# A recurrent layer with an FFN gate on one core: the gate computed in the preparation, and each super-tile finished inside the next one

## The chip, the cores and the metric

The kernel runs on one core of one Trainium2 chip. A core has four compute engines that run side by side and meet at semaphores: TensorE (PE; its weight loads are listed as PEld), VectorE (DVE), ScalarE (ACT) and GpSimd (POOL); SyncE (SP) issues the DMA transfers here. SBUF and PSUM are its memories. The metric is the time of the whole program on the device in microseconds (us); the median of three runs is given.

## The reference

The input x is (4, 1024, 128), 4096 tokens of 128 features. All is float32.

```python
xn = layernorm(x)
s  = attn(xn)                       # H=32 heads, P=64, N=64, DI=2048
x  = x + s * silu(ffn(xn))

# attn
proj = u @ in_proj_w.T              # z, xin, B, C, dt, theta, lambda
Bm = rms(Braw) * w + B_bias         # per head; Cm likewise
tc = cumsum(theta, axis=1)          # over the tokens
Bm, Cm = rope(Bm, tc), rope(Cm, tc) # v1*cos - v2*sin, v1*sin + v2*cos
h  = a_t * h + g_t * (x_t B_t) + b_t * (x_{t-1} B_{t-1})   # per head, a scan
y  = h C_t + xh * D
y  = rms(y * silu(z)) * norm_w
return y @ out_proj_w.T

# ffn: both operands through fp8 with one scale for each tensor
fake_quant(t) = fp8(t * 448 / max|t|) * max|t| / 448
ffn = fake_quant(xn) @ fake_quant(weight).T + bias
```

The gate needs the largest magnitude of the whole of xn. The RMS norm of y runs over all 32 heads of a token, and it is a factor per token behind the output projection.

## The kernel before, in words

The 4096 tokens are cut into 8 super-tiles (t) of 512 tokens, a super-tile into 4 chunks of 128. The 32 heads go in 8 groups (q) of 4 heads; each group is two pairs (p). Three functions run one after the other, each a block with a barrier at its end; inside a block each engine has its own list of instructions, in the order in which they are written.

`prepare` (stage 1) normalises x, transposes it (`xnT`) and the weights, takes the running sum of xn over the tokens (`tcT`, since the angle is linear in it), and computes B and C, the decays and the per-token factors (`kk`, `cc`, `dec`, `cum`). `xnT`, `tcT`, B/C and the decays are stored to DRAM (`xn_t`, `tc_t`, `bc_t`, `cum_parts`, `cum_rows`). VectorE works through chains of whole-width operations (L484 to L543); ScalarE makes the transposed B/C (L604), the logarithms and exponentials (L615 to L628) and the casts (L635 to L643).

`units` (stage 2) is the recurrence, 64 rounds (t, q). For each:
- angle: TensorE `angles` (L825), ScalarE `rounding` (L1122), VectorE `angles` (L1000) to a fraction of a turn; ScalarE `sines` (L1126 to L1133) fill `tri`, and SP's `spread` (L774), eight DMAs, lays them out over the partitions of `trig`. This is done for round q + 2 during q, and a spread of pair p waits until VectorE has read the old `trig`.
- rotation (L1026): eight VectorE operations, each (B or C + bias) x (cos or sin); GpSimd's `sums` (L1189) add them in pairs to `rot`. This is done one round ahead.
- TensorE transposes the rotated B (L836), makes exponents (L846, L853), scores (L864), states (L916), x (L830), z (L944), y (L950 to L966) and the output projection (L878), which adds up over q in one PSUM bank, `Op`. ScalarE exponentiates (L1138, L1160), applies Silu to z (L1164) and squares (L1143); VectorE scales x (L1010), masks scores (L1044), updates the state (L1075), multiplies y by silu(z) (L1103) and decays B (L1036); GpSimd makes `ce` (L1198) and adds the squares over the heads in `sqa` (L1220).
- At the end of a super-tile TensorE sums `sqa` over the features (L987) into the bank `Dp`; ScalarE copies `Op` to `s_acc` (L1175) and the sums to `ssq` (L1177). At q = 2 VectorE takes the largest and the smallest of this super-tile's xn (`mags`, L1109).
- Before the first round, angles, sines and spreads for q = 0 and 1 are made with nothing beside them.

`finish` (stage 3) turns `mags` into the fp8 scales, `ssq` into 1/rms, and passes over the 8 super-tiles again: xn and x are loaded, ScalarE scales xn twice (L1309, L1310), VectorE rounds it to fp8 in five steps (`quantise`, L1363 to L1369), TensorE multiplies with the weight, VectorE adds the bias (L1389), ScalarE takes tanh (L1315), VectorE completes Silu and multiplies (L1395, L1398), GpSimd scales `s_acc` (L1407) and adds x (L1415), and SP stores the result.

## Time and profile before

| | us |
|---|---|
| median of 3 runs | 1339.04 (1335.22 to 1344.77) |
| the profiled execution | 1338.07 |
| its span, first to last instruction | 1336.3 |

| engine | busy us | share of the span |
|---|---|---|
| VectorE | 1224.1 | 92% |
| TensorE, matmuls | 1133.7 | 85% |
| TensorE, weight loads | 832.9 | 62% |
| ScalarE | 797.7 | 60% |
| GpSimd | 728.3 | 55% |

Each engine's busy time is its instructions' time added up; an average over the three stages hides that they have different limits. The last stage runs from 1271.7 on, the first up to 98.0.

### The profile page before, as it was taken

How to read it: one execution, taken by the hardware profiler on the slowest of the kernel's cores; microseconds unless marked ns; L12 is line 12 of the kernel's file. 1: busy time of each engine (PE TensorE's matmuls, PEld its weight loads, DVE VectorE, ACT ScalarE, POOL GpSimd, SP SyncE). 2: the span in 40 equal slices, each digit the busy share in tenths (PEclk: the TensorE clock that was granted, in tenths of full speed). 3: DMA queues.
4: the chain of work that ended last, by engine and by line, in shares of the span. 5: the costliest groups of instructions: out<-in, count | busy, mean ns of one | idle time of the engine just before them, and what ended most of it. 6: DMA issues, size and time to landing. Idle time of an engine off the chain costs nothing. (4 is left out here: it accounts for less than half of the span.)

```text
span 1336.3 us, 30910 instructions
## 1 busy us (share of the span) xinstructions
PE 1133.7 (85%) x11514; PEld 832.9 (62%) x11514; DVE 1224.1 (92%) x1945; ACT 797.7 (60%) x1226; POOL 728.3 (55%) x562
## 2 busy tenths in 40 slices
PE   4873999989999999999999999899999999999810
PEld 3742666666666666666676666666766666667600
DVE  7774999989998999999998999899989999999688
ACT  5732666656666666666666666666666666666432
POOL 4001566656665566556664666566655665666523
PEclk9865999999999999999999999999999999999955
DMA  7535332343221422342223323342224323222033
GB/s 185 176 98 127 73 73 65 69 93 85 65 65 44 106 66 66 68 112 66 63 63 74 81 66 68 66 113 57 60 51 112 66 65 69 61 57 60 19 100 89
DMA packets 68513, 105.66 MB, mean 79 GB/s; under 512 B 14051, under 2 KB 32716, under 8 KB 68044
## 3 DMA queue, kind: packets, MB, share of 16 engines
q1 hardware_dynamic: 68364, 103.68, 33.2%
q8 instruction: 93, 1.52, 0.5%
q14 instruction: 56, 0.46, 0.1%
HBM read 24.73 MB, written 9.96 MB: 26 GB/s over the span
## 5 line engine op out<-in xcount | busy, mean ns | idle before, releaser
L1189 POOL TENSOR_TENSOR rot<-part 128x512 f32<-128x512 f32 x256 | 382.5, 1494 | 531.9 <-DVE part L1026 480.4
L1026 DVE SCALAR_TENSOR_TENSOR part<-bcs,k_prmT,trig 128x512 f32<-128x512 f32 x512 | 500.5, 1028 | 1.4 <-DMA trig<-tri 1.3
L1138 ACT ACTIVATE E<-d 128x512 f32<-128x512 f32 x256 | 151.7, 592 | 184.1 <-PE d L846 181.5
L864 PE MATMUL s<-rot 64*128 64x128 f32 x2048 | 149.7, 285 | 23.6 <-POOL rot L1189 19.1
L1044 DVE TENSOR_TENSOR M<-s,E 128x512 f32<-128x512 f32 x256 | 163.5, 678 | 2.4 <-PE s L864 1.8
L864 PEld LDWEIGHTS s<-rot 64*128 64x128 f32 x2048 | 126.9, 188 | 62.0 <-issue 54.6
L1198 POOL TENSOR_TENSOR ce<-rot,eb 128x512 f32<-128x512 f32 x128 | 160.1, 1272 | 3.0 <-ACT eb L1160 3.0
L1220 POOL TENSOR_TENSOR sqa<-sqa,sq 128x512 f32<-128x512 f32 x112 | 142.5, 1272 | 14.2 <-ACT sq L1143 6.2
L956 PE MATMUL y<-M,xk 128*64 128x128 f32 x2048 | 140.1, 279 | 0.0
L878 PEld LDWEIGHTS o<-k_w_o,yT 128*128 128x128 f32 x1024 | 132.5, 191 | 10.4 <-DVE yT L1103 5.0
L878 PE MATMUL o<-k_w_o,yT 128*128 128x128 f32 x1024 | 134.5, 275 | 2.6 <-DVE yT L1103 2.6
L830 PE MATMUL r<-k_w_zx,xns 128*128 128x256 f32 x512 | 133.2, 382 | 3.3 <-DVE ang L1000 3.3
L944 PE MATMUL r<-xns,k_w_zx 128*128 128x512 f32 x256 | 122.6, 596 | 4.2 <-DVE xc L1010 4.2
L956 PEld LDWEIGHTS y<-M,xk 128*64 128x64 f32 x2048 | 109.2, 136 | 21.5 <-issue 21.5
L825 PE MATMUL r<-tcs,k_w_th 128*128 128x512 f32 x128 | 73.9, 660 | 56.6 <-DVE bw L1036 42.3
L1160 ACT ACTIVATE eb<-d 128x512 f32<-128x512 f32 x128 | 76.5, 597 | 68.4 <-PE d L853 68.4
L1164 ACT ACTIVATE sz<-r 128x512 f32<-128x512 f32 x128 | 76.4, 597 | 61.1 <-PE r L944 60.9
L1143 ACT ACTIVATE sq<-yT 128x512 f32<-128x512 f32 x128 | 80.0, 625 | 48.9 <-DVE yT L1103 48.9
L1010 DVE TENSOR_TENSOR xk<-r,k_kk 128x512 f32<-128x512 f32 x128 | 88.0, 688 | 22.6 <-PE r L830 22.0
L830 PEld LDWEIGHTS r<-k_w_zx,xns 128*128 128x128 f32 x512 | 96.9, 192 | 15.8 <-issue 4.8
L846 PE MATMUL d<-k_cum,k_pick 111*128 111x512 bf16 x256 | 99.6, 389 | 0.0
L916 PEld LDWEIGHTS r<-xk,bw 128*64 128x64 f32 x1792 | 57.5, 137 | 50.7 <-DVE bw L1036 44.4
(234 smaller groups left out, 1792.8 us busy)
## 6 DMA issues: line engine op xcount, KB each, us to landing
trig<-tri SPq DMA_DIRECT2D x512, 128.0 KB, 2.4
bcs<-bc_t SPq DMA_DIRECT2D x16, 256.0 KB, 4.0
bcs<-bc_t SPq DMA_DIRECT2D x32, 128.0 KB, 3.9
a_big<-in_L_attn_u SPq DMA_DIRECT2D x4, 512.0 KB, 6.0
xn_t<-a_xnT SPq DMA_DIRECT2D x1, 2048.0 KB, 16.4
tc_t<-a_tcT SPq DMA_DIRECT2D x1, 2048.0 KB, 15.9
bc_t<-a_tmp SPq DMA_DIRECT2D x1, 2048.0 KB, 7.5
tcs<-tc_t SPq DMA_DIRECT2D x8, 256.0 KB, 3.0
```

What stands on the lines that cost most here:

```text
L830: last = nc.tensor.matmul(R[i][:, 256 * c:256 * c + 256], xns[:, (t + q // NQ) % 2, (2 * i + c) * P:(2 * i + c + 1) * P], K["w_zx"][:, DI ...
L846: nc.tensor.matmul(Dp[:], K["pick"][:, head * P:head * P + P], K["cum"][0:D_ROWS, q % 2, h, :], start=True, stop=True).then_inc(d_ready, 1)
L864: last = nc.tensor.matmul(Sp[j][:, k], rot[rows, q % 2, p, 0, k], rot[rows, q % 2, p, 1, k], start=True, stop=True)
L878: last = nc.tensor.matmul(Op[:, k], yT[:, p, k], K["w_o"][:, (2 * q + p) * P:(2 * q + p + 1) * P], start=False, stop=q == NQ - 1 and c == ...
L944: nc.tensor.matmul(R[p][:], w, xns[:, t % 2, :], start=True, stop=True).then_inc(z_ready, 1)
L956: nc.tensor.matmul(Yp[p][m:m + 64, k], xk[:, par, c, 128 * p + m:128 * p + m + 64], M[:, 2 * p + j, k], start=False, stop=c == 0 and begin ...
L1026: nc.vector.scalar_tensor_tensor(out=part[:, 2 * p + f, :], in0=bcs[:, (t + q // NQ) % 2, 2 * w + f, :], scalar=col, in1=trig[:, p, 1 - f, ...
L1044: nc.vector.tensor_tensor(M[:, h, :], Sp[h % 2][:], E[:, h % 2, :], ALU.mult).then_inc(m_ready, 1)
L1138: nc.scalar.activation(E[:, h % 2, :], Dp[:], ACT.Exp).then_inc(e_ready, 1)
L1189: nc.gpsimd.tensor_tensor(rot[:, q % 2, p, w, :], part[:, 2 * p, :], part[:, 2 * p + 1, :], ALU.add).then_inc(rot_ready, 1)
L1198: nc.gpsimd.tensor_tensor(ce[:, p, :], rot[:, q % 2, p, 1, :], eb[:, p, :], ALU.mult).then_inc(ce_ready, 1)
L1220: nc.gpsimd.tensor_tensor(sqa[:], sqa[:], sq[:, p, :], ALU.add).then_inc(sqa_ready, 1)
```

## The change

- **Gate in `prepare`.** VectorE takes the largest and the smallest of `xnT` (`extreme`, eight reductions over 1024 columns) and of the FFN weight, and makes the scales (`sc`). ScalarE scales xn (`gate_input`), VectorE quantises (`quantise`, the same five steps), TensorE multiplies, with the bias put in as a first matmul, and ScalarE applies Silu directly. The eight gates are stored to DRAM (`gate_rows`) at the end of the stage.
- **Angles of q = 0 and 1 in `prepare`.** Two matmuls on `tcT`, rounding, fraction and sines; group 0 is also spread. `rnd` shares memory with `tcT`, so the first rounding waits until `tcT` has been stored (`stored[1]`).
- **`units` starts with the loads of B/C**; the first rotations come ahead of the scaling of x.
- **`units` finishes super-tile t - 1 during t.** At q = 0: VectorE reads the sums of squares (`norm_start`), ScalarE takes the root (`root`), VectorE the reciprocal (`norm_seeded`), GpSimd refines it (`norm_refined`), ScalarE copies `Op` with the factor for each token (`normalised`). At the end of q = 1 GpSimd multiplies by the gate and adds x (`finished`); SP stores at q = 2 and loads the next gate and x at q = 4. For the last super-tile VectorE does the two products.
- **Gone:** `finish`, `s_acc`, `ssq`, `mags` with its reductions at q = 2, ScalarE's two copies at a super-tile's end and GpSimd's wait there.

Three places as they stand in the engines' lists. First ScalarE in the preparation, from the exponentials to the first transposed B/C (`a_tmp`), before:

```order
L615 ACTIVATE a_s<-a_s 128x1024
L616 ACTIVATE a_s<-a_dl 128x1024
L604 ACTIVATE a_tmp<-a_ps,a_wnc 128x512 x2
L620 ACT_TABLE_LOAD
L620 ACTIVATE a_s<-a_s 128x1024
L604 ACTIVATE a_tmp<-a_ps,a_wnc 128x512 x2
```

and now:

```order
L734 ACTIVATE a_s<-a_s 128x1024
L735 ACTIVATE a_s<-a_dl 128x1024
L739 ACTIVATE a_tcT<-a_psx,k_cols 128x512
L723 ACTIVATE a_tmp<-a_ps,a_wnc 128x512 x2
L743 ACT_TABLE_LOAD
L743 ACTIVATE a_s<-a_s 128x1024
L723 ACTIVATE a_tmp<-a_ps,a_wnc 128x512 x2
```

The rounding of the first angle (`a_tcT` from `a_psx`) now stands ahead of all eight transposed copies.

Second, VectorE at q = 0 of super-tile 1 (`part` are the rotations, `ang` the angle of q = 2, `hs` the states, `M` the masked scores), before:

```order
L1026 SCALAR_TENSOR_TENSOR part<-bcs,k_prmT,trig 128x512
L1000 SCALAR_TENSOR_TENSOR ang<-rnd,r 128x512
L1075 SCALAR_TENSOR_TENSOR hs<-k_carry,k_dtot,r 128x64 x2
L1075 SCALAR_TENSOR_TENSOR hs<-hs,k_dtot,r 128x64 x4
L1026 SCALAR_TENSOR_TENSOR part<-bcs,k_prmT,trig 128x512
L1010 TENSOR_TENSOR xk<-r,k_kk 128x512
L1010 TENSOR_TENSOR xc<-r,k_cc 128x512
L1010 TENSOR_TENSOR xk<-r,k_kk 128x512
L1010 TENSOR_TENSOR xc<-r,k_cc 128x512
L1044 TENSOR_TENSOR M<-s,E 128x512 x2
L1026 SCALAR_TENSOR_TENSOR part<-bcs,k_prmT,trig 128x512 x6
```

and now:

```order
L1207 SCALAR_TENSOR_TENSOR part<-bcs,k_prmT,k_trig 128x512
L1231 TENSOR_SCALAR nrm<-d 128x4
L1181 SCALAR_TENSOR_TENSOR ang<-rnd,r 128x512
L1266 SCALAR_TENSOR_TENSOR hs<-k_carry,k_dtot,r 128x64 x2
L1266 SCALAR_TENSOR_TENSOR hs<-hs,k_dtot,r 128x64 x4
L1207 SCALAR_TENSOR_TENSOR part<-bcs,k_prmT,k_trig 128x512
L1191 TENSOR_TENSOR xk<-r,k_kk 128x512
L1191 TENSOR_TENSOR xc<-r,k_cc 128x512
L1191 TENSOR_TENSOR xk<-r,k_kk 128x512
L1191 TENSOR_TENSOR xc<-r,k_cc 128x512
L1225 TENSOR_TENSOR M<-s,E 128x512 x2
L1236 RECIPROCAL nrm<-nrm 128x4
```

The read of the sums (`nrm` from `d`) has come in ahead of the angle, and the reciprocal behind the scores.

Third, ScalarE in the same round (`E` and `eb` are exponentials, `sz` Silu, `tri` sines, `sq` squares), before:

```order
L1175 COPY k_s_acc<-o 128x512
L1177 COPY k_ssq<-d 128x4
L1122 ACTIVATE rnd<-r,k_cols 128x512
L1138 ACTIVATE E<-d 128x512 x2
L1160 ACTIVATE eb<-d 128x512 x2
L1164 ACT_TABLE_LOAD
L1164 ACTIVATE sz<-r 128x512 x2
L1126 ACTIVATE rnd<-ang 128x512
```

and now:

```order
L1325 ACTIVATE rnd<-r,k_cols 128x512
L1340 ACTIVATE E<-d 128x512 x2
L1373 ACTIVATE eb<-d 128x512 x2
L1351 ACT_TABLE_LOAD
L1351 ACTIVATE nrm<-nrm 128x4
L1379 ACT_TABLE_LOAD
L1379 ACTIVATE sz<-r 128x512 x2
L1329 ACTIVATE rnd<-ang 128x512
L1332 ACTIVATE k_tri<-ang 128x512
```

The two copies at the start are gone; a table load and the root have come in ahead of the Silu, whose table is loaded behind it as before. The four copies `so` follow at the end of the round.

```diff
...
+def spread(sp, K, p, landed):
+    for j in range(2):
+        h = 2 * p + j
+        for d in range(2):
+            r = 64 * j + 32 * d
+            sp.dma_start(K["trig"][r:r + 32, p, :, :], K["tri"][32 * h:32 * h + 32, d:3:2 - d, :]).then_inc(landed, 16)
...
+            sp.wait_ge(sin_done, 3)
+            for p in range(2):
+                spread(sp, K, p, dup_stored)
...
+            for t in range(NS):
+                sp.wait_ge(g_done, t + 1)
+                sp.dma_start(gate_d[t], fgate[:, t % 2, :]).then_inc(gate_stored[t % 2], 16)
...
+            nc.tensor.matmul(ps_x[0][:], K["w_th"][:, 0:P], tcT[:, 0:ST], start=True, stop=True).then_inc(u_t, 1)
...
+            nc.tensor.matmul(ps[5][:], K["w_th"][:, P:2 * P], tcT[:, 0:ST], start=True, stop=True).then_inc(u_t, 1)
...
+            for t in range(NS):
+                b = ps[2 + t % 2]
+                if t >= 2:
+                    pe.wait_ge(g_done, t - 1)
+                nc.tensor.matmul(b[:], ones[0:1, :], bias4[:], start=True, stop=False, skip_group_check=True)
+                pe.wait_ge(xq_done, t + 2)
+                for c in range(CS):
+                    last = nc.tensor.matmul(b[:, c * P:c * P + P], xq[:, t % 2, c * P:c * P + P], wq[:], start=False,
+                                            stop=c == CS - 1, skip_group_check=True)
+                last.then_inc(g_t, 1)
...
+                link(nc.vector.tensor_reduce(peak[:, i, b:b + 1], xnT[:, b * L:(b + 1) * L], AX.X, op))
...
                 nc.vector.tensor_copy(big[:, 512 * g:512 * g + 512], ps[B_BANK[g]][:]).then_inc(bc_copied_v, 1)
+                extreme(g // 2, ALU.max)
...
+            extreme(0, ALU.min)
+            extreme(1, ALU.min)
             dve.wait_ge(stored[1], 16)
...
+            dve.wait_ge(rounded, 1)
+            nc.vector.scalar_tensor_tensor(out=ang, in0=rnd, scalar=MAGIC, in1=ps_x[0][:],
+                                           op0=ALU.subtract, op1=ALU.subtract).then_inc(turned, 1)
+            extreme(2, ALU.min)
+            extreme(3, ALU.min)
...
+            wpeak = st32[:, 5, 2 * BATCH:2 * BATCH + 2]
+            link(nc.vector.tensor_reduce(wpeak[:, 0:1], stage2[:, 10 * P:11 * P], AX.X, ALU.max))
...
+            dve.wait_ge(w_scaled, 2)
+            quantise(wq[:], wv[:, 0, :], wv[:, 1, :], P)
...
+            nc.vector.scalar_tensor_tensor(out=ang, in0=rnd, scalar=MAGIC, in1=ps[5][:],
+                                           op0=ALU.subtract, op1=ALU.subtract).then_inc(turned, 1)
...
-            link(nc.vector.tensor_reduce(K["mags"][:, 2 * NS:2 * NS + 1], stage2[:, 10 * P:11 * P], AX.X, ALU.max))
-            link(nc.vector.tensor_reduce(K["mags"][:, 2 * NS + 1:2 * NS + 2], stage2[:, 10 * P:11 * P], AX.X, ALU.min))
+            for t in range(NS):
+                dve.wait_ge(xq_done, t + 1)
+                dve.wait_ge(x_scaled, 2 * t + 2)
+                if t >= 2:
+                    dve.wait_ge(g_t, t - 1)
+                quantise(xq[:, t % 2, :], fv[:, t % 2, :], fmag[:, t % 2, :], ST)
...
+            act.wait_ge(u_t, 1)
+            act.wait_ge(stored[1], 16)
+            act.wait_ge(exp_done, 2)
+            nc.scalar.activation(rnd, ps_x[0][:], ACT.Identity, bias=K["cols"][:, 1:2]).then_inc(rounded, 1)
...
+            def gate_input(t):
+                if t >= 2:
+                    act.wait_ge(xq_done, t)
+                for dst, f in ((fv, ACT.Copy), (fmag, ACT.Abs)):
+                    nc.scalar.activation(dst[:, t % 2, :], xnT[:, t * ST:(t + 1) * ST], f, scale=sc[:, 0:1]).then_inc(x_scaled, 1)
...
+            sines(0)
+            act.wait_ge(sc_done, 2)
+            for i, f in enumerate((ACT.Copy, ACT.Abs)):
+                nc.scalar.activation(wv[:, i, :], w_ffn[:], f, scale=sc[:, 1:2]).then_inc(w_scaled, 1)
+            act.wait_ge(pr_done, 1)
+            act.wait_ge(bcT_t, 8)
+            gate_input(0)
+            gate_input(1)
...
+            sines(1)
+            for t in range(NS):
+                if t + 2 < NS:
+                    gate_input(t + 2)
+                act.wait_ge(g_t, t + 1)
+                if t >= 2:
+                    act.wait_ge(gate_stored[t % 2], 16 * (t // 2))
+                nc.scalar.activation(fgate[:, t % 2, :], ps[2 + t % 2][:], ACT.Silu, scale=sc[:, 5:6]).then_inc(g_done, 1)
...
+            def load_finish(t):
+                if t > 0:
+                    sp.wait_ge(gated, t)
+                    sp.wait_ge(o_stored, 16 * t)
+                sp.dma_start(gate[:], gate_d[t]).then_inc(gate_loaded, 16)
+                sp.dma_start(by_chunk(res), u_v[t]).then_inc(res_loaded, 16)
+            def store(t):
+                sp.wait_ge(o_ready, t + 1)
+                sp.dma_start(o_v[t], by_chunk(res)).then_inc(o_stored, 16)
+            load_bc(0)
+            sp.dma_start(xns[:, 0, :], xn_d[0]).then_inc(xn_loaded, 16)
             sp.dma_start(tcs[:, 0, :], tc_d[0]).then_inc(tc_loaded, 16)
-            sp.dma_start(xns[:, 0, :], xn_d[0]).then_inc(xn_loaded, 16)
-            load_bc(0)
...
-            spread(0, 0)
-            spread(0, 1)
+            for p in range(2):
+                sp.sem_inc(dup[p], DUP)
+            spread_next(0, 1)
...
-                        sp.wait_ge(mags_done, at(2, t, 0))
                         sp.dma_start(xns[:, (t + 1) % 2, :], xn_d[t + 1]).then_inc(xn_loaded, 16)
+                    if q == 2 and t > 0:
+                        store(t - 1)
+                    if q == 4:
+                        load_finish(t)
...
+            def norm_start(t):
+                dve.wait_ge(ssq_ready, at(1, t, 1))
+                dve.wait_ge(norm_ready, t)
+                nc.vector.tensor_scalar(nrm[:, 0, :], Dp[:, 0:CS], 1.0 / DI, EPS, ALU.mult, ALU.add).then_inc(ssq_taken, 1)
+            def norm_seeded(t):
+                dve.wait_ge(root_done, t + 1)
+                nc.vector.reciprocal(nrm[:, 1, :], nrm[:, 2, :]).then_inc(norm_seed, 1)
             for w in range(2):
+                if w == 1:
+                    x_scaled(0, 0, 0, 0)
+                    x_scaled(0, 0, 0, 1)
                 for p in range(2):
...
+                    if q == 0 and t > 0:
+                        norm_start(t - 1)
...
+                    if q == 0 and t > 0:
+                        norm_seeded(t - 1)
...
-                    if q == 2:
-                        dve.wait_ge(xn_loaded, (t + 1) * 16)
-                        for i, op in enumerate((ALU.max, ALU.min)):
-                            nc.vector.tensor_reduce(K["mags"][:, t * 2 + i:t * 2 + i + 1], xns[:, t % 2, :], AX.X, op).then_inc(mags_done, 1)
...
+            norm_start(NS - 1)
+            norm_seeded(NS - 1)
+            dve.wait_ge(acc_done, at(1, NS, 0))
+            dve.wait_ge(gate_loaded, 16 * NS)
+            nc.vector.tensor_tensor(so[:], so[:], gate[:], ALU.mult).then_inc(gated, 1)
+            dve.wait_ge(gated, NS)
+            dve.wait_ge(res_loaded, 16 * NS)
+            nc.vector.tensor_tensor(res[:], so[:], res[:], ALU.add).then_inc(o_ready, 1)
...
-            rounding(0, 0)
-            sines(0, 0, first=True)
-            rounding(0, 1)
-            sines(0, 1)
+            def root(t):
+                act.wait_ge(ssq_taken, at(1, t, 1))
+                act.wait_ge(norm_seed, t)
+                nc.scalar.activation(nrm[:, 2, :], nrm[:, 0, :], ACT.Sqrt).then_inc(root_done, 1)
+            def normalised(t):
+                act.wait_ge(out_ready, at(T1, t, T1))
+                act.wait_ge(norm_ready, t + 1)
+                act.wait_ge(o_ready, t)
+                for c in range(CS):
+                    last = nc.scalar.activation(so[:, c * P:c * P + P], Op[:, c * P:c * P + P], ACT.Copy, scale=nrm[:, 1, c:c + 1])
+                last.then_inc(acc_done, 1)
...
+                    if q == 0 and t > 0:
+                        root(t - 1)
...
-                act.wait_ge(out_ready, at(T1, t, T1))
-                nc.scalar.copy(K["s_acc"][:, t * ST:t * ST + ST], Op[:]).then_inc(acc_done, 1)
-                act.wait_ge(ssq_ready, at(1, t, 1))
-                nc.scalar.copy(K["ssq"][:, t * CS:t * CS + CS], Dp[:, 0:CS]).then_inc(ssq_taken, 1)
+                    if q == 0 and t > 0:
+                        normalised(t - 1)
+            root(NS - 1)
+            normalised(NS - 1)
...
+            def norm_refined(t):
+                r, v = nrm[:, 1, :], nrm[:, 0, :]
+                pool.wait_ge(norm_seed, t + 1)
+                nc.gpsimd.tensor_tensor(tch[:], r, r, ALU.mult).then_inc(nch, 1)
+                pool.wait_ge(nch, 3 * t + 1)
+                nc.gpsimd.tensor_tensor(tch[:], tch[:], v, ALU.mult).then_inc(nch, 1)
+                pool.wait_ge(nch, 3 * t + 2)
+                nc.gpsimd.tensor_scalar(tch[:], tch[:], -0.5, 1.5, ALU.mult, ALU.add).then_inc(nch, 1)
+                pool.wait_ge(nch, 3 * t + 3)
+                nc.gpsimd.tensor_tensor(r, r, tch[:], ALU.mult).then_inc(norm_ready, 1)
+            def finished(t):
+                pool.wait_ge(acc_done, at(1, t, 1))
+                pool.wait_ge(gate_loaded, 16 * (t + 1))
+                nc.gpsimd.tensor_tensor(so[:], so[:], gate[:], ALU.mult).then_inc(gated, 1)
+                pool.wait_ge(gated, t + 1)
+                pool.wait_ge(res_loaded, 16 * (t + 1))
+                nc.gpsimd.tensor_tensor(res[:], so[:], res[:], ALU.add).then_inc(o_ready, 1)
...
-                pool.wait_ge(ssq_ready, at(1, t, 0))
...
+                    if q == 0 and t > 0:
+                        norm_refined(t - 1)
...
                         nc.gpsimd.tensor_tensor(sqa[:], sqa[:], sq[:, p, :], ALU.add).then_inc(sqa_ready, 1)
-
-
-def finish(nc, K, u, xn_d, out):
...
```

## Rows read from the trace of the kernel before

**Rows 1.** Windows: us, busy us (instructions) of PE, PEld, DVE, ACT, POOL, clock, DMA, GB/s.
```profile
0.00:98.00 98.00, 66.77 (x399) 54.72 (x399) 74.01 (x82) 52.13 (x92) 16.45 (x42) 0.84 0.54 151
134.70:1266.00 1131.30, 1044.72 (x11017) 764.56 (x11016) 1078.03 (x1757) 715.04 (x1087) 683.27 (x498) 1.00 0.31 70
1271.70:1336.30 64.60, 5.51 (x35) 3.12 (x35) 55.92 (x87) 18.65 (x29) 19.73 (x16) 0.52 0.33 98
```

**Rows 2.** Timeline, closing stage: start, duration, engine, line, operation, names, [idle before].
```profile
1280.18 0.43 DVE L1363 TENSOR_SCALAR f_half<-f_v 128x512 fp8e4<-128x512 f32 x1
1283.28 0.43 DVE L1363 TENSOR_SCALAR f_half<-f_v 128x512 fp8e4<-128x512 f32 x1
```

**Rows 3.** Timeline, start-up of the recurrence.
```profile
103.95 1.06 SPq L763 DMA_DIRECT2D bcs<-bc_t  x2
118.82 8.40 DVE L1026 SCALAR_TENSOR_TENSOR part<-bcs,k_prmT,trig 128x512 f32<-128x512 f32 x8
128.61 1.97 PE L836 MATMUL r<-k_ident,rot 128*128 128x128 f32 x8 [11.04 <-POOL rot L1189]
```

**Rows 4.** Timeline, boundary between super-tiles 0 and 1.
```profile
276.21 1.05 PE L987 MATMUL d<-k_ones,sqa 128*128 128x1 f32 x8 [0.78 <-POOL sqa L1220]
278.99 0.69 DVE L1000 SCALAR_TENSOR_TENSOR ang<-rnd,r 128x512 f32<-128x512 f32 x1 [2.28 <-ACT rnd L1122]
```

**Rows 5.** Groups by shape, VectorE and ScalarE: busy us, mean ns, idle before.
```profile
L427 DVE TENSOR_REDUCE a_st<-a_big 128x8 f32<-128x1024 f32 x4 | 4.9, 1213 | 4.9 <-DMA a_big<-in_L_attn_u 4.9
...
L598 ACT ACTIVATE k_w_o<-a_ps,k_prmT 128x128 f32<-128x128 f32 x16 | 4.6, 368 | 0.4
```

**Rows 6.** Timeline, preparation, first part.
```profile
58.48 0.69 ACT L604 ACTIVATE a_tmp<-a_ps,a_wnc 128x512 f32<-128x512 f32 x1 [1.90 <-PE a_ps L375]
63.85 2.29 DVE L493 TENSOR_TENSOR a_tcT<-a_big 128x2048 f32<-128x2048 f32 x1 [2.44 <-issue]
```

**Rows 7.** Timeline, end of preparation.
```profile
85.93 1.22 DVE L521 TENSOR_TENSOR a_s<-a_s,a_cum 128x1024 f32<-128x1024 f32 x1 [3.53 <-ACT a_cum L641]
95.48 0.29 DVE L543 TENSOR_REDUCE k_mags<-a_stage 128x1 f32<-128x128 f32 x1
98.00 1.09 SPq L777 DMA_DIRECT2D tcs<-tc_t  x1
```

**Rows 8.** Timeline at q = 2 of super-tile 0.
```profile
186.56 1.26 DVE L1109 TENSOR_REDUCE k_mags<-xns 128x1 f32<-128x512 f32 x2
187.74 1.27 DVE L1044 TENSOR_TENSOR M<-s,E 128x512 f32<-128x512 f32 x2
```

**Rows 9.** Timeline at q = 0 of super-tile 1.
```profile
283.70 1.28 ACT L1164 ACT_TABLE_LOAD   x1
284.99 0.60 ACT L1164 ACTIVATE sz<-r 128x512 f32<-128x512 f32 x1
286.35 6.09 DVE L1026 SCALAR_TENSOR_TENSOR part<-bcs,k_prmT,trig 128x512 f32<-128x512 f32 x6
286.46 0.60 ACT L1164 ACTIVATE sz<-r 128x512 f32<-128x512 f32 x1 [0.87 <-PE r L944]
290.18 5.12 SPq L774 DMA_DIRECT2D trig<-tri  x8
295.96 0.73 DVE L1026 SCALAR_TENSOR_TENSOR part<-bcs,k_prmT,trig 128x512 f32<-128x512 f32 x1
```

**Rows 10.** Timeline at q = 1 to 2 of super-tile 1.
```profile
311.15 2.68 POOL L1220 TENSOR_TENSOR sqa<-sqa,sq 128x512 f32<-128x512 f32 x2
313.32 1.06 DVE L1026 SCALAR_TENSOR_TENSOR part<-bcs,k_prmT,trig 128x512 f32<-128x512 f32 x1
317.19 1.27 POOL L1189 TENSOR_TENSOR rot<-part 128x512 f32<-128x512 f32 x1 [3.36 <-DVE part L1026]
```

**Rows 11.** Timeline, the last sum of squares and the last product.
```profile
1271.31 0.16 ACT L1177 COPY k_ssq<-d 128x4 f32<-128x4 f32 x1 [1.23 <-PE d L987]
...
1332.32 1.26 POOL L1415 TENSOR_TENSOR f_o<-f_sr,f_xin 128x512 f32<-128x512 f32 x1 [0.63 <-DVE f_sr L1398]
```

335 lines of the change are left out of this document (124 added, 211 removed).

## The prediction

> **What bounds the kernel now.** I read the stage windows first, then the timeline of each seam, then the costs by shape. The windows [rows 1] cut the span of 1336.3 us into preparation (98.0 us), start-up of the recurrence (36.7 us, the slow first group), steady recurrence (1131.3 us) and the closing stage (64.6 us). In the steady stage VectorE is busy 1078.0 of 1131.3 us, 95%, so it is the bound there: taking an operation from VectorE is worth its length, adding one elsewhere costs nothing unless VectorE has to wait for it. In the closing stage VectorE is busy 55.9 of 64.6 us while the others idle. Its repeating piece is the five-step quantising of one super-tile, 1280.18 to 1283.28, which is 3.10 us when GpSimd is silent [rows 2]. In the start-up nothing is busy: the first rotation comes at 118.82, 20.8 us after the first load at 98.00, and TensorE's first matmul on its result at 128.61, 30.6 us after it [rows 3]. At a super-tile's boundary VectorE idles 2.28 us for the angle of the next group: TensorE does the sum of squares (276.21, 1.05 us), then the angle matmul, ScalarE rounds (0.69), and VectorE goes on at 278.99 [rows 4].
>
> **Preparation grows.** In order on VectorE:
> - Eight reductions over 1024 columns, 1.21 us each as such reductions take now [rows 5], 9.7 us. Four stand between copies that wait for ScalarE about 1.1 us each, two in the 2.44 us that VectorE waits for the store of the sums [rows 6]. That hides 1.1 x 3 + 2.4 = 5.7; 4.0 us lie on its path.
> - Two angles at 0.69 [rows 4]: 1.4. Twelve tiny ones (peaks, scales) at 0.2 to 0.3, the bias row among them: 3.4. The two reductions of the FFN weight, 0.29 each [rows 7], only move. Quantising the weight: 1.4, for which its 128 columns cost less than half of the 3.10.
> - VectorE waits 3.53 us for ScalarE's cast near the end [rows 7]. The weight's quantising stands just there, and what delays VectorE alone shortens that wait: 3.5 come back.
> Sum: 4.0 + 1.4 + 3.4 + 1.4 - 3.5 = 6.7 us. ScalarE gives the same from its side: its rounding must wait for the store of the sums, which ends at about 63.8, where VectorE too resumed at 63.85; its transposed copies began at 58.48, and now begin after the 0.69 us rounding at 64.5, 6.0 us later, and with them, in ScalarE's order, the logarithms and exponentials on which VectorE's chain leans [rows 6]. The two delays overlap: I take 6.3, between them.
> - Then eight super-tiles of the gate on VectorE, 8 x 3.10 = 24.8 us [rows 2]. GpSimd has no work there. ScalarE needs 2.0 us for each (two scalings, one Silu), TensorE 0.6: both hidden.
> - Before, 2.2 us lay between VectorE's end (95.77) and the next stage's first load (98.00) [rows 7]. Now behind the last quantising come TensorE 0.6, ScalarE 0.6, a store with its end (2.7, the last product's end at 1333.58 to the span's end) [rows 11] and the barrier, 0.6: 4.5. Plus 2.3.
> Preparation: +6.3 + 24.8 + 2.3 = **+33.4 us**, the next stage at about 131.4. Bounds: every stage perfectly covered, +28; nothing covered, +40.
>
> **Start-up shrinks.** Rounding, sines and spread of group 0 are gone from it, and group 1's sines too. The six loads of the B and C rows now go first: 3.6 us of issues, as at 101.47 to 105.01, and 3.9 to land, so the first rotation stands at 7.5 after the stage's start. Eight rotations take 8.4 us [rows 3] with the four scalings of x (0.69 each, 2.7) in the middle, and GpSimd's last sum 1.3: 7.5 + 8.4 + 2.7 + 1.4 = 20.0 where 30.6 stood. **-10.6 us.** Bounds -14 (loads land at once) and -6 (the load of x, now second, holds the scalings). Group 1's spread starts behind the sixth rotation and is landed 5 us later, before VectorE returns to it.
>
> **The steady stage.** Removed: two reductions at each q = 2; from the first to what follows is 1.18 us [rows 8]; eight times 9.4. Some of it comes back as waits: without the reductions VectorE comes that much earlier to the x products, which read TensorE's work. I keep 8. Added on VectorE: the norm start, inside the 2.28 us idle [rows 4], free; a reciprocal of 0.2 in seven tiles, 1.4. ScalarE: the copies of output and sum of squares leave the boundary, but the angle matmul, not they, release the rounding, so the 2.28 us stay. Added at q = 0: a table load and a root between the exponentials and Silu, 1.28 + 0.23 = 1.5 us. The second Silu waited 0.87 for TensorE, so 0.7 us is left; four operations of 0.6 to 0.7 stand between the Silu's end at 287.06 and the last sine, which ends at some 290.0 instead of 289.3. The spread started at 290.18, when VectorE had read the old table (its fourth rotation of the six from 286.35), so it doesn't move [rows 9]. Four scaled copies, of which sixteen take 4.6 us, so 1.2 us [rows 5], at the end of q = 0 push the next rounding 0.3 us; VectorE has the rotation before it. GpSimd: its two products of 1.27 follow the sums that end at 313.83; its next sum is at 317.19 after 3.36 us idle [rows 10]; 2.6 us fit. A rotation beside GpSimd takes 1.06 instead of 0.74 [rows 10]; between 313.9 and 316.5 VectorE's other work reads PSUM, and 0.69 us of it beside GpSimd is no longer than elsewhere. At most one rotation is met: 0.3 in seven tiles, 2.0, of which I take half. SP gets two loads and a store per tile, 0.5 us of issue each; the eight spreads of a group hold it 5.1 of about 17.5 us [rows 9], so there is room, and the store waits for GpSimd's second product at 316.5, ahead of what SP does next. Sum: -8 + 1.4 + 1.0 = -5.6, in round **-6 us**. Bounds: -16 (9.4, and half of the boundary's 7 x 2.28, with ScalarE's copies gone) and +8 (2 us of new waits a tile).
> The Trainium skill, SBUF — State Buffer, "Who interferes with whom", says that a VectorE operation with two SBUF inputs and a GpSimd one that reads SBUF block each other for the whole instruction. By that a product of 1.27 us could cost VectorE its full length in each of seven tiles, 9 us in all and a time of 1306, inside the forecast's own band below; the row of 1.06 us shows 0.3 for a meeting.
>
> **The closing stage goes.** The last sum of squares is taken at 1271.31 [rows 11]. From there: norm start 0.2, root 0.25 (its table is loaded in the wait), reciprocal 0.2, four GpSimd operations on 128x4, which no row shows: the nearest row is ScalarE's 128x4 copy, 0.16 [rows 11], the farthest a whole 128x512 sum, 1.27 [rows 10], so 0.6 to 5 with 0.1 between them; near the small one, 1.2; four scaled copies 1.2 [rows 5]; product and sum 1.4; store to the end 2.7 [rows 11]. 7.2 to the end instead of 65.0: **-57.8 us** (-54 to -58.5).
>
> **Sum.** 33.4 - 10.6 - 6.0 - 57.8 = -41.0; span 1336.3 - 41.0 = 1295.3. The profiled execution took 1338.07, 1.8 above its span: 1297.1. The median shown is 1339.04, 1.0 above that execution: about **1298 us**, 3% less.
>
> **Rivals.**
> 1. The forecast: 1287 to 1308, chance 0.68.
> 2. An extra switch of ScalarE's table costs more than its load. For: it is added at seven tiles, ahead of the sines. Against: in the rows ScalarE goes straight on behind a load: the load of 1.28 us at 283.70 has its Silu at 284.99 [rows 9]. If each of two switches took 1.4 more, the sines would end at 292.8, the spread's first four issues and landing 4.9 later, 297.7, and VectorE, due at 295.96 [rows 9], would wait 1.7; seven tiles 12 us: 1310. Chance 0.08. The Trainium skill, ScalarE: Activation LUTs, "What ACT_TABLE_LOAD costs", has a drain of about 1380 ns behind each load; the trace does not show it.
> 3. The gate's loop in preparation is not VectorE's 3.10 us but a round through three engines, as in the closing stage, where a super-tile cost 64.6 / 8 = 8.1 with other work [rows 1]. Halfway, 5 us each: +15, 1313. Chance 0.06.
> 4. The boundary frees itself: with ScalarE's copies gone the 2.28 us shrink and fewer waits answer the removed reductions. 7 x 1.5 = 10 less: 1288 down to 1281. Chance 0.15.
> 5. Slower: the norm start is put in VectorE's queue ahead of angles, state and all else, and waits for TensorE's sum of squares, which waits for GpSimd's last sum. VectorE stands if the matmul ends after 278.99 instead of 277.26 [rows 4]: from 1.7 us late every us is paid seven times. To lose the 41 us it must be 7.6 us late in each tile: 1345. GpSimd is busy only 683 of 1131 us [rows 1], so chance 0.01. Other mishaps 0.02.
>
> **Numbers.** The likeliest is 1298. The range reaches into rivals 2 and 4 and takes the bounds of preparation and start-up: 1284 to 1312. A measurement here can tell about 1% (13 us) from no change: faster needs less than 1326: 0.97; same 0.02; slower 0.01.
>
> **What would show it.** Preparation ending near 131; eight quantisings of 3.1 us back to back; ScalarE's first transposed copy at 64.5; TensorE's first use of a rotation 20 us after the stage's start; no reductions at q = 2; boundary idle of VectorE still 2.3 us; the trig table's spread at q = 0 still behind the fourth rotation, with no VectorE wait on it; two GpSimd products inside the idle after q = 1; 7 us from the last sum of squares to the end. The forecast is wrong if VectorE shows waits of over 1 us per tile on the spread or the sum of squares, or if the gate's loop takes over 4 us a super-tile.

## The result and the profile after

The changed kernel takes 1302.70 us (median, 1299.14 to 1303.54); beside it the kernel before took 1339.39 (1335.22 to 1344.77). The ratio is 0.9724 [0.9704, 0.9745]: 2.8% less. Forecast were 1298 and 1284 to 1312. The profiled execution took 1303.54, its span is 1301.8 where 1336.3 stood: 34.5 us less, forecast 41.0. By seam:

| part | forecast | measured | from |
|---|---|---|---|
| preparation | +33.4 | +35.1 | next stage at 133.08, was 98.00 |
| start-up, to TensorE's first rotation | -10.6 | -11.4 | 152.32 - 133.08 = 19.2, was 30.6 |
| steady stage | -6 | -0.4 | first rotation of group 1 to last sum of squares: 1134.96, was 1135.38 |
| closing | -57.8 | -57.8 | 7.2, was 65.0 |

The four add up to -34.5. The first fence has windows of the changed kernel (columns as in [rows 1]): preparation, steady stage, and what is left of the closing.

```profile
0.00:133.08 133.08, 90.21 (x454) 62.68 (x454) 111.17 (x149) 78.67 (x131) 16.45 (x42) 0.78 0.50 142
158.50:1294.50 1136.00, 1049.03 (x11041) 767.95 (x11040) 1068.35 (x1757) 728.46 (x1118) 716.25 (x542) 1.00 0.34 76
1294.60:1301.80 7.20, 0.00 (x0) 0.00 (x0) 1.72 (x4) 1.34 (x5) 0.79 (x4) 0.55 0.13 36
```

The steady stage has kept its length although VectorE has less to do. From the first decayed B rows (`bw`) to the last, VectorE is busy 1064.6 us of 1122.7, where it was busy 1075.5 of 1123.1: 10.9 less work, 10.5 more idle. Of the idle, 9.2 us are one new wait at the seven boundaries, which mostly stands where longer rotations stood; the sections below take it apart. That is the one term that was wrong in kind.

The preparation, timeline (start, duration, engine, line, operation, names, [idle before]). ScalarE's rounding waits for the store of the time sums; VectorE waits for the scales' matmul; then the quantising runs at 3.10 us a tile; after its end come TensorE, ScalarE, the store and the next stage, 4.05 us in all.

```profile
65.12 0.69 ACT L739 ACTIVATE a_tcT<-a_psx,k_cols 128x512 f32<-128x512 f32 x1 [6.79 <-DMA tc_t<-a_tcT]
65.70 0.68 ACT L723 ACTIVATE a_tmp<-a_ps,a_wnc 128x512 f32<-128x512 f32 x1
...
84.14 0.16 DVE L593 TENSOR_SCALAR a_sc<-a_psx 128x2 f32<-128x2 f32 x1 [2.14 <-PE a_psx L423]
...
104.27 0.43 DVE L618 TENSOR_SCALAR a_half<-a_big 128x512 fp8e4<-128x512 f32 x1
...
107.37 0.43 DVE L618 TENSOR_SCALAR a_half<-a_big 128x512 fp8e4<-128x512 f32 x1
...
128.34 0.69 DVE L624 SCALAR_TENSOR_TENSOR a_xq<-a_half,a_big 128x512 bf16<-128x512 fp8e4 x1
129.09 0.60 PE L461 MATMUL a_ps<-a_wq,a_xq 128*128 128x128 bf16 x4 [0.49 <-DVE a_xq L624]
129.74 0.69 ACT L809 ACTIVATE a_big<-a_ps,a_sc 128x512 f32<-128x512 f32 x1 [2.41 <-PE a_ps L461]
130.45 0.32 SPq L239 DMA_DIRECT2D gate_rows<-a_big  x1
133.08 0.65 SPq L928 DMA_DIRECT2D bcs<-bc_t  x1
```

The start-up, which answers to [rows 3]: the first rotation now waits for the loads of B and C alone.

```profile
141.13 3.75 DVE L1207 SCALAR_TENSOR_TENSOR part<-bcs,k_prmT,k_trig 128x512 f32<-128x512 f32 x4 [12.10 <-DMA bcs<-bc_t]
152.32 1.97 PE L1019 MATMUL r<-k_ident,rot 128*128 128x128 f32 x8 [6.93 <-POOL rot L1403]
```

The boundary between super-tiles 0 and 1, VectorE and then GpSimd, which answers to [rows 4, 9]. Of the old idle of 2.28 us, 0.60 is now ahead of the norm's first step and 1.52 ahead of the angle; with the 0.16 of the step itself that is 2.28 again, so the norm start was free. The reciprocal in front of the rotations puts them back by 0.09. New is the 1.31 in the middle of the six rotations.

```profile
300.76 0.16 DVE L1231 TENSOR_SCALAR nrm<-d 128x4 f32<-128x4 f32 x1 [0.60 <-PE d L1167]
302.44 0.69 DVE L1181 SCALAR_TENSOR_TENSOR ang<-rnd,r 128x512 f32<-128x512 f32 x1 [1.52 <-ACT rnd L1325]
...
309.90 2.71 DVE L1207 SCALAR_TENSOR_TENSOR part<-bcs,k_prmT,k_trig 128x512 f32<-128x512 f32 x4
313.92 2.40 DVE L1207 SCALAR_TENSOR_TENSOR part<-bcs,k_prmT,k_trig 128x512 f32<-128x512 f32 x2 [1.31 <-POOL rot L1403]
```

```profile
310.06 0.62 POOL L1418 TENSOR_TENSOR tch<-nrm 128x4 f32<-128x4 f32 x1 [1.00 <-DVE nrm L1236]
310.75 0.58 POOL L1420 TENSOR_TENSOR tch<-tch,nrm 128x4 f32<-128x4 f32 x1
311.43 0.57 POOL L1422 TENSOR_SCALAR tch<-tch 128x4 f32<-128x4 f32 x1
312.08 0.58 POOL L1424 TENSOR_TENSOR nrm<-nrm,tch 128x4 f32<-128x4 f32 x1
312.62 2.49 POOL L1403 TENSOR_TENSOR rot<-part 128x512 f32<-128x512 f32 x2
```

The four small operations keep GpSimd from its sums until 312.62, VectorE has filled its part buffers by then, and stands until the first sum is done. The round is only some 0.35 us longer for it, not 1.31: before, the fourth of these rotations stood beside a sum and took 1.77 us (288.34 to 290.11, inside the 6.09 of [rows 9]); now it takes 0.74. The closing, which answers to [rows 11], has the same four at a third of the length each:

```profile
1294.59 0.16 DVE L1231 TENSOR_SCALAR nrm<-d 128x4 f32<-128x4 f32 x1 [3.96 <-PE d L1167]
1294.79 0.21 ACT L1351 ACTIVATE nrm<-nrm 128x4 f32<-128x4 f32 x1 [2.19 <-DVE nrm L1231]
...
1295.28 0.20 POOL L1418 TENSOR_TENSOR tch<-nrm 128x4 f32<-128x4 f32 x1 [1.83 <-DVE nrm L1236]
...
1296.41 1.14 ACT L1359 ACTIVATE so<-o,nrm 128x128 f32<-128x128 f32 x4 [1.41 <-POOL nrm L1424]
1297.58 0.69 DVE L1309 TENSOR_TENSOR so<-so,gate 128x512 f32<-128x512 f32 x1 [2.38 <-ACT so L1359]
...
1299.02 0.41 SPq L949 DMA_DIRECT2D out<-res  x1
```

**A ruler for the steady stage.** VectorE's first product of each round (the decayed B rows, L1217) marks it. The distance from one to the next repeats within some 0.02 us from tile to tile in nearly all rounds, so it shows tenths that a median of runs would not. Rounds in us, even and odd super-tiles (a boundary is counted with the tile that ends); in the other rounds the two kernels agree within 0.02, but for single ones that are up to 0.15 off, and for the two named below:

| round | before | after | difference |
|---|---|---|---|
| that with the two reductions | 18.12 / 17.99 | 17.42 / 17.19 | -0.70 / -0.79 |
| across a boundary | 20.31 / 20.55 | 20.74 / 20.97 | +0.43 / +0.42 |
| that with GpSimd's products, odd tiles | 17.20 | 17.32 | +0.12 |

In sum: -6.0 for eight tiles, +3.0 for seven boundaries, +0.5 for four odd tiles, +0.5 in the first round, and +1.5 in one round of the last tile, where the granted clock falls to 1.2 GHz for some 3.4 us, right behind a wait of TensorE of 1.44 us: -0.5, against -0.4 measured. That wait is in the round behind each of the seven boundaries; only here did the clock fall. It comes back under the refinement of the root.

```profile
1172.00:1174.00 2.00, 1.68 (x2) 0.37 (x2) 2.00 (x5) 1.76 (x6) 1.19 (x1) 0.62 0.78 165
1174.00:1176.00 2.00, 2.00 (x26) 1.47 (x25) 1.56 (x4) 0.69 (x1) 0.08 (x1) 0.52 0.33 71
```

### The profile page after: what moved, and what is told of

Same layout as the page of the kernel before. It is cut to its first block and busy times, and to the rows that moved or that the text cites. A ratio compares the mean times of both kernels' runs of the same rounds, so it can differ in the third digit from the quotient of the medians.

```text
span 1301.8 us, 30976 instructions
## 1 busy us (share of the span) xinstructions
PE 1149.1 (88%) x11530; PEld 837.3 (64%) x11530; DVE 1193.7 (92%) x1925; ACT 811.0 (62%) x1257; POOL 739.4 (57%) x592
## 3 DMA queue, kind: packets, MB, share of 16 engines
q8 instruction: 93, 1.52, 0.5%
## 5 line engine op out<-in xcount | busy, mean ns | idle before, releaser
L1403 POOL TENSOR_TENSOR rot<-part 128x512 f32<-128x512 f32 x256 | 375.8, 1469 | 515.6 <-DVE part L1207 515.6
L1207 DVE SCALAR_TENSOR_TENSOR part<-bcs,k_prmT,k_trig 128x512 f32<-128x512 f32 x512 | 495.9, 1017 | 22.7 <-DMA bcs<-bc_t 12.1
L1013 PE MATMUL r<-k_w_zx,xns 128*128 128x256 f32 x512 | 133.1, 382 | 12.1 <-DMA xns<-xn_t 12.1
L1061 PEld LDWEIGHTS o<-k_w_o,yT 128*128 128x128 f32 x1024 | 132.5, 191 | 10.5 <-DVE yT L1298 5.0
L1013 PEld LDWEIGHTS r<-k_w_zx,xns 128*128 128x128 f32 x512 | 97.5, 192 | 23.1 <-DMA xns<-xn_t 12.4
L1008 PE MATMUL r<-tcs,k_w_th 128*128 128x512 f32 x124 | 71.0, 655 | 46.9 <-DVE bw L1217 46.9
```

What stands on the lines that cost most here:

```text
L1013: last = nc.tensor.matmul(R[i][:, 256 * c:256 * c + 256], xns[:, (t + q // NQ) % 2, (2 * i + c) * P:(2 * i + c + 1) * P], K["w_zx"][:, DI ...
L1061: last = nc.tensor.matmul(Op[:, k], yT[:, p, k], K["w_o"][:, (2 * q + p) * P:(2 * q + p + 1) * P], start=False, stop=q == NQ - 1 and c == ...
L1207: nc.vector.scalar_tensor_tensor(out=part[:, 2 * p + f, :], in0=bcs[:, (t + q // NQ) % 2, 2 * w + f, :], scalar=col, in1=trig[:, p, 1 - f, ...
L1403: nc.gpsimd.tensor_tensor(rot[:, q % 2, p, w, :], part[:, 2 * p, :], part[:, 2 * p + 1, :], ALU.add).then_inc(rot_ready, 1)
```

## Experiments

Four questions: what the reductions were worth, what ate their gain, whether the gate's loop lies wholly on the path, and which of the parts (gate, tables, overlap) earned the 34.5 us. Where a kernel ran only once, the seams and rounds of its trace decide, not its time.

### The reductions put back

```diff
+                    if q == 2:
+                        dve.wait_ge(xn_loaded, (t + 1) * 16)
+                        for i, op in enumerate((ALU.max, ALU.min)):
+                            nc.vector.tensor_reduce(mags[:, t * 2 + i:t * 2 + i + 1], xns[:, t % 2, :], AX.X, op).then_inc(mags_done, 1)
```

> The changed kernel with the two maximum/minimum reductions (128x512) put back into VectorE's queue, in round 2 of every super-tile, at their old place; their result is not used. Theory A, the forecast's price: they cost what they last, 8 pairs of 1.2 us, so the span goes from 1301.8 to 1311.4 us and the round that holds them from 17.4 to 18.6 us. Theory B, read from the rounds of the two traces: VectorE waits for x at that place anyway (0.2 to 0.4 us a wait), and a pair costs 0.70 us in an even tile and 0.79 in an odd one: the span is 1307.8 us, and the round that holds them is 18.1 us in an even tile and 18.0 in an odd one.

Measured: 1309.66 us (1307.47 to 1312.93), ratio 0.9792 [0.9752, 0.9832]. The round that holds them: 18.12 in even, 17.99 in odd tiles, the kernel before's sizes to the hundredth and those of theory B: 6.0 us over eight tiles. (The span, 1305.8, is lower than either theory's since the first round, at another clock, took 19.4 us instead of 20.9.) But theory B's reason is the smaller half of the truth. A pair delays what follows by 1.18 us; where 0.4 of that goes back to is seen in the first rotation behind it, in the same round of super-tile 1, of the changed kernel and then of this one:

```profile
354.52 1.07 DVE L1207 SCALAR_TENSOR_TENSOR part<-bcs,k_prmT,k_trig 128x512 f32<-128x512 f32 x1
...
352.35 2.69 POOL L1456 TENSOR_TENSOR sqa<-sqa,sq 128x512 f32<-128x512 f32 x2
```

```profile
354.42 0.73 DVE L1210 SCALAR_TENSOR_TENSOR part<-bcs,k_prmT,k_trig 128x512 f32<-128x512 f32 x1
```

Without the reductions VectorE reaches the rotation 1.2 us earlier, while GpSimd still adds up squares (to 355.04), and the rotation takes 1.07 us instead of 0.73; with them it comes after the sums. That is 0.33 in every tile. The wait for x puts its reader back by up to 0.25 in even tiles (an idle of 0.17 where there was none) and by 0.07 at most in odd ones.

### The refinement of the root left out, and moved

```diff
-                nc.gpsimd.tensor_tensor(tch[:], r, r, ALU.mult).then_inc(nch, 1)
...
-                nc.gpsimd.tensor_tensor(r, r, tch[:], ALU.mult).then_inc(norm_ready, 1)
+                pool.sem_inc(norm_ready, 1)
```

> The changed kernel without GpSimd's four 128x4 operations that refine the reciprocal root (the seed is used as it is). Theory A: these four, 2.6 us beside VectorE's rotations, stand in GpSimd's queue ahead of the next rotations and make VectorE wait 1.3 us for a free part buffer; without them the round across a tile boundary goes back from 20.74 us to the 20.31 of the kernel before, 7 times 0.43, and the closing loses 1.3 us: span about 1297.5. Theory B: the boundary costs more because VectorE's first step of the norm waits 0.6 us for the sum of squares in its queue; then the round stays at 20.7 and only the closing gets shorter: span about 1300.5.

One run: 1301.77 us, span 1300.1. The boundary rounds are 20.38 (even) and 20.62 (odd): 0.35 of the 0.43 is GpSimd's four operations, theory A, and some 0.07 the reciprocal on VectorE. The closing is 1.1 us shorter, 6.15 instead of 7.23. The six rotations are in one piece again:

```profile
312.08 0.17 DVE L1236 RECIPROCAL nrm<-nrm 128x4 f32<-128x4 f32 x1
312.16 6.07 DVE L1207 SCALAR_TENSOR_TENSOR part<-bcs,k_prmT,k_trig 128x512 f32<-128x512 f32 x6
```

The expected 4.3 us are not in the span, since this execution's next stage begins at 136.3 instead of 133.1 with the same preparation; more of that below. Then the same operations kept, but moved:

```diff
-                    if q == 0 and t > 0:
-                        norm_refined(t - 1)
                     if live(t, q + 1):
                         for k in range(1, 4):
                             sums(t, q + 1, k)
+                    if q == 0 and t > 0:
+                        norm_refined(t - 1)
...
                         rounding(t, q + 2)
+                    if q == 1 and t > 0:
+                        normalised(t - 1)
...
-                    if q == 0 and t > 0:
-                        normalised(t - 1)
```

> The changed kernel with GpSimd's four operations of the norm behind the rotations of their round, and ScalarE's scaling of the finished tile one round later. Theory A: they then meet nothing that VectorE waits for: the round across a boundary goes from 20.74 us (even tiles) and 20.97 (odd) to 20.38 and 20.62, as with the four left out, 2.5 us in all. Theory B: ScalarE's 1.1 us for the finished tile stands in front of the decays that VectorE waits for in the next round, and takes the gain back: boundary round at 20.4, the one behind it 0.4 us or more longer.

One run: 1297.35 us, span 1295.6. Boundary rounds 20.38 and 20.61, as with the four left out; the round behind it is 17.55 instead of 17.37 in odd tiles and unchanged in even ones. Both theories hold a part: 7 x 0.36 less, 4 x 0.18 more, 1.8 us net. (The rest of the 6 us is an earlier next stage, at 131.5, a shorter first round, and no fall of the clock in the steady stage.)

That last item may be the refinement's too. Since GpSimd's sums come later behind it, TensorE stands longer in the next round, ahead of the angle matmul. The same place in the changed kernel and in the one without the refinement:

```profile
1172.32 1.94 PE L1008 MATMUL r<-tcs,k_w_th 128*128 128x512 f32 x2 [1.44 <-DVE bw L1217]
```

```profile
1173.13 1.12 PE L1008 MATMUL r<-tcs,k_w_th 128*128 128x512 f32 x2 [0.77 <-DVE bw L1217]
```

Nine profiled executions (the changed kernel's and those of eight experiments) have the refinement at its place, and there TensorE stands 1.43 or 1.44 us behind all 63 boundaries; behind 13 of these the granted clock fell for 3.4 us, at 1.5 us each. In the other five (the kernel before, the refinement left out or moved, the overlap undone, the edits together) it stands 0.77 us, and behind none of 35 did it fall. Why it fell behind 13 and not behind the other 50 is open, and no run changes this wait alone.

### The gate for two tiles instead of eight

```diff
-            for t in range(NS):
+            for t in range(2):
                 dve.wait_ge(xq_done, t + 1)
```

> The changed kernel with the gate's quantising, matmuls and Silu done for two of the eight super-tiles only (the rows of the others are stored from the second's). Theory A, the forecast's: each tile's five VectorE operations, 3.10 us, lie wholly on the path of the preparation: 6 times 3.10 = 18.6 us less, next stage at 114.5 us instead of 133.1, span 1283.2. Theory B: under the gate loop lies another chain (the second table's sines, the copies and stores of the cumulated rows) that ends late too, so less than 12 us comes back and the next stage begins after 121 us.

Measured: 1288.12 us (1286.17 to 1290.37), ratio 0.9623 [0.9589, 0.9657]. VectorE's loop runs from 103.38 to 109.55, so 6 x 3.10 us are gone, and nothing else was waiting under it: theory A for the loop. The next stage begins at 117.75 rather than 114.5, because the six extra stores of one tile's rows are issued in a bunch behind the last Silu, 8.2 us from VectorE's end to the stage instead of 4.05. That belongs to this experiment, not to the change. (Six of the eight gates are not computed here, so the result is not the program's.)

### The overlap undone, the gate left in the preparation

```diff
+                act.wait_ge(out_ready, at(T1, t, T1))
+                nc.scalar.copy(acc[:, t * ST:t * ST + ST], Op[:]).then_inc(acc_done, 1)
...
+            for t in range(NS):
...
+                nc.vector.tensor_tensor(so2[:, i, :], so2[:, i, :], gate2[:, i, :], ALU.mult).then_inc(pdd, 1)
+                dve.wait_ge(pdd, t + 1)
+                nc.vector.tensor_tensor(so2[:, i, :], so2[:, i, :], res2[:, i, :], ALU.add).then_inc(o_ready, 1)
```

> The changed kernel with its overlap undone and nothing else: the gate is still made in the preparation and the start is the changed one, but the projected tiles and their sums of squares are kept, and norm, gate product, residual sum and store of all eight super-tiles come behind the last one, two buffers deep. Theory A: the overlap is worth a stage of its own; each tile needs a load of gate and residual, 1.1 us of ScalarE, 1.4 of VectorE and a store, some 4 to 5 us a tile bound by the transfers, so the closing is 35 to 45 us instead of 7.2 and the time 1328 to 1338. Theory B: what made the old closing long was the quantising (8 times 3.1 us and its scales), and without it eight tiles go by at VectorE's 1.4 us each: closing under 20 us, time about 1312.

Measured: 1327.18 us (1326.63 to 1328.18), ratio 0.9915 [0.9883, 0.9948]. From the last sum of squares at 1288.2 to the end 38.1 us: theory A. VectorE is busy 12.27 of them and waits for the residual's load in each tile from the third on, about 4.3 us a tile:

```profile
1288.20:1326.30 38.10, 0.00 (x0) 0.00 (x0) 12.27 (x22) 11.78 (x35) 0.00 (x0) 0.53 0.49 138
```

```profile
1313.51 0.69 DVE L1317 TENSOR_TENSOR part<-part,bcs 128x512 f32<-128x512 f32 x1 [2.85 <-DMA bcs<-in_L_attn_u]
1314.23 0.69 DVE L1319 TENSOR_TENSOR part<-part,bcs 128x512 f32<-128x512 f32 x1
1317.81 0.69 DVE L1317 TENSOR_TENSOR part<-part,bcs 128x512 f32<-128x512 f32 x1 [2.89 <-DMA bcs<-in_L_attn_u]
```

The boundary rounds are 20.32 and 20.55 again, the old ones. So the 57.8 us of the closing fall in two: 65.0 - 38.1 = 26.9 for the gate's work that left it, and 38.1 - 7.2 = 30.9 for the overlap, which costs 3.0 at the boundaries and 0.5 for the products. By the spans the overlap earned 1326.3 - 1301.8 = 24.5 us of the 34.5.

The other 10.0 us (1336.3 to 1326.3) are there without it: the preparation is 33.8 longer, the start-up 11.1 shorter, the steady stage 5.8 (the reductions) and the closing 26.9. The median says the same: 0.9915, and its interval ends below 1. Of these 10 us the tables have about one, as the next experiment shows; the rest, about nine, goes with the move of the gate. On the closing alone it would be a loss, 26.9 gained for some 30 paid. It pays by what goes with it: the reductions (6) and the stores that its loop puts far ahead of the next stage's loads (4.5 to 6, see below).

The 24.5 us are measured against this closing, with two buffers and one SyncE queue, where the next load is issued only when an earlier store has ended. For two thirds of its 38.1 us VectorE is idle; a better closing behind the last tile, at VectorE's 12.3 us, was not built, and against it the overlap would be worth less.

### The tables made at the old place

```diff
-            pe.wait_ge(tc_done, 1)
-            nc.tensor.matmul(ps_x[0][:], K["w_th"][:, 0:P], tcT[:, 0:ST], start=True, stop=True).then_inc(u_t, 1)
...
+            rounding(0, 0)
+            sines(0, 0, first=True)
+            rounding(0, 1)
+            sines(0, 1)
```

> The changed kernel with one part undone: the first two head groups' angles, sines and spreads are made at the start of the next stage again, in the old order, and not in the preparation. Theory A, the forecast's sum: the preparation gets back 6.3 us and the start loses 10.6, so the next stage begins at 126.8 us, the first TensorE use of the rotations stands 30.6 us behind it, and the span is 1306. Theory B, from the changed kernel's trace: the tables' chain cost the preparation nearer 9 us (first quantising at 104.3 us where 95.1 stood) and saved 11.4, so the next stage begins at 124 us, and the span is 1304, within the spread of the runs. Theory C: the tables cost nothing in the preparation, since what made its chain longer is the scale of the gate; then the next stage stays at 133 and the span is 1313.

Measured: 1304.64 us (1303.20 to 1306.62), ratio 0.9740 [0.9714, 0.9767], beside 0.9724 with the tables in the preparation: no difference that can be told. The next stage begins at 128.72, 4.4 us earlier, and its start takes 24.6 us, 5.4 longer than 19.2. The tables so cost the preparation 4.4 us against this execution of the changed kernel. Measured from VectorE's same step in the preparation (first of L551) to the quantising, which leaves out what an execution was ahead before, they cost 3.0 to 5.8 against six executions with the tables there at the same clock, 3.6 in the middle. None of the theories had the second number: the old order of work, back in place, does not give the old 30.6 back. The first load, issued at 128.72, reaches TensorE at 131.40; in the kernel before it was issued at 98.00 and TensorE ran at 105.27. Ahead of it there, 0.6 us after their issue, stood the stores of the cumulated rows. That was put to the test by putting these stores behind the gate's rows:

```diff
+            for t in range(NS):
+                sp.wait_ge(g_done, t + 1)
+                sp.dma_start(gate_d[t], fgate[:, t % 2, :]).then_inc(gate_stored[t % 2], 16)
             sp.wait_ge(cumT_a, 2)
             sp.wait_ge(cumT_v, 2)
...
-            for t in range(NS):
-                sp.wait_ge(g_done, t + 1)
-                sp.dma_start(gate_d[t], fgate[:, t % 2, :]).then_inc(gate_stored[t % 2], 16)
```

> The kernel of the run in which the first tables are made at the start of the next stage again, with one more change: the stores of the cumulated rows are issued behind the gate's rows, directly ahead of the next stage's first load, as in the kernel before. Theory A: those stores hold the first load back: it landed 2.7 us behind the stage's start without them ahead and 7.3 us in the kernel before, so here the first TensorE use of the rotations goes from 24.6 us behind the stage's start to 28 or more. Theory B: the start became shorter for another reason, and it stays at 24.6 us.

One run: 1315.97 us. The stage's first load is issued at 131.60, TensorE's first angle matmul comes 6.8 us later, at 138.39, and the first use of a rotation at 160.67, 29.1 us behind the stage's start: theory A.

```profile
138.39 2.08 PE L981 MATMUL r<-tcs,k_w_th 128*128 128x512 f32 x2 [12.85 <-DMA tcs<-tc_t]
160.67 1.97 PE L992 MATMUL r<-k_ident,rot 128*128 128x128 f32 x8 [11.04 <-POOL rot L1383]
```

(Of the 11.4 us by which the span is longer than with the tables alone put back, 4.5 are this, 2.9 a later next stage behind the same stores, and nearly all the rest is three falls of the clock in the steady stage where the other execution had one, and one late spread.) So of the 11.4 us that the start got shorter, 4.5 come from the gate's loop, which stands between the stores and the next stage's loads. Another 1.5 remain between 29.1 and 30.6: ScalarE's table for the sines is loaded already, so that no 1.28 us load stands ahead of them as it did at 109.47 in the kernel before; no run takes that apart. Only 5.4 come from the tables, which cost the preparation 4.4.

### Ways to a shorter preparation

A buffer of its own for the first rounded angles:

```diff
-        rnd, ang = tcT[:, 5 * ST:6 * ST], dl[:, 3 * ST:4 * ST]
+        rnd, ang = sb("a_rnd", [P, ST])[:], dl[:, 3 * ST:4 * ST]
```

> The changed kernel with a buffer of its own for the first rounded angles, so that ScalarE's first rounding does not wait for the store of the time sums (6.8 us of idle, the wait that ends at 65.1 us). Theory A: ScalarE's transposed copies begin 6 us earlier and the whole chain with them: next stage at 127 to 129 us instead of 133.1, span 1296 to 1298. Theory B: VectorE's product waits for the same store at the same time, so the chain keeps its time whatever ScalarE does: under 2 us at the next stage's start.

One run: 1304.28 us. The rounding stands at 57.62 instead of 65.12, but the first quantising at 101.22, 3.1 earlier, and the next stage at 130.02: between the theories. Of the 3.1, 0.8 is not the edit's: VectorE reached the same step ahead of it (first of L551) at 57.00 instead of 57.80. VectorE's wait for the scales' matmul has gone with the late copies: it was 2.14 us, and here, as in the run with the tables at the old place, it is 0.03.

```profile
80.75 0.16 DVE L593 TENSOR_SCALAR a_sc<-a_psx 128x2 f32<-128x2 f32 x1
```

> The changed kernel with the matmul that spreads the gate's scales over the partitions put ahead of the last group of linear terms in TensorE's queue. Theory A: VectorE's wait of 2.1 us for it (ends at 84.1 us) goes, and the first quantising starts 2 us earlier, at 102.2 us. Theory B: VectorE's chain waits for the same linear terms a little later anyway, and the start of the quantising stays within 0.5 us of 104.3 at the same TensorE clock.

One run (the edit moves one matmul between two groups): 1303.93 us. VectorE's wait for the scales is 0.48 instead of 2.14, and in the six executions at the same clock with the matmul at its old place and late copies it was 1.75 to 2.18: the wait is shorter by the edit. The first quantising stands at 102.72. That is theory A's direction, but by its time it is not told apart from chance: seven executions with an untouched preparation up to that loop (the changed kernel's and those of six experiments) begin it at 102.7, 103.0, 103.4, 103.4, 104.3, 105.6 and 107.5. For the latest of them the trace shows the clock, at the same instructions: the same stretch with TensorE without a pause, at 2.4 GHz in the changed kernel's execution and at 1.2 GHz in the one without the refinement. Behind it VectorE is at the step L551 at 63.3 instead of 57.8. The execution of 105.6 had 2.4 GHz there, as the others; its reason is open.

```profile
34.00:48.00 14.00, 14.00 (x127) 13.41 (x125) 11.35 (x14) 8.62 (x16) 0.00 (x0) 1.00 0.39 104
```

```profile
34.00:48.00 14.00, 14.00 (x69) 14.00 (x69) 5.87 (x7) 3.59 (x7) 0.00 (x0) 0.51 0.38 99
```

Splitting the gate's loop:

```diff
+                nc.scalar.activation(halves[:, t % 2, :], xnT[:, t * ST:(t + 1) * ST], ACT.Copy, scale=sc[:, 6:7], saturate=False).then_inc(x_scaled, 1)
...
+                nc.gpsimd.tensor_scalar(smalls[:, t % 2, :], fv[:, t % 2, :], 24576.0, -24576.0, ALU.add, ALU.add).then_inc(seeded, 1)
```

> The changed kernel with the gate's five VectorE operations a tile split over three engines: the rounding by halves is written by ScalarE from the scaled input, the first sum by GpSimd, and VectorE keeps three. Theory A: VectorE bounds the loop, so a tile goes from 3.10 to 2.2 us (0.73 + 0.73 + 0.69), 7.4 us less, next stage at 125.7 us, span 1294. Theory B: ScalarE, with four passes of 0.6 us and the Silu beside a wait, is the next bound at 2.6 to 3.0 us a tile: less than 4 us is gained. Theory C: the handing over between engines costs more than it saves, and a tile takes over 3.1 us.

Measured: 1303.22 us (1302.90 to 1303.37), ratio 0.9728 [0.9708, 0.9748]: nothing. In the trace the loop takes 21.8 us instead of 24.8, and ScalarE repeats every 2.72 us without a pause but 0.20: theory B, ScalarE is the next bound. But the loop began at 108.0, again with the lower clock from 34 to 48 us, and so the gain is not in this execution's time. Whether the other three had that clock too is not on record, so why the median shows nothing stays open.

```profile
122.10 1.33 ACT L772 ACTIVATE a_big<-a_xnT,a_sc 128x512 f32<-128x512 f32 x2 [0.20 <-DVE a_xq L636]
123.34 0.70 ACT L773 ACTIVATE a_halves<-a_xnT,a_sc 128x512 fp8e4<-128x512 f32 x1
123.95 0.67 ACT L823 ACTIVATE a_big<-a_ps,a_sc 128x512 f32<-128x512 f32 x1
```

> The changed kernel with the six first loads of the next stage's B and C rows issued by two engines, three by SyncE and three by ScalarE, instead of six in a row. Theory A: the issue bounds the start: the last of the six is issued 1.8 us earlier, the first rotation stands 6.3 us behind the stage's start instead of 8.05, and the span is 1300. Theory B: the transfers bound it: the rotation stays at 8 us and nothing is gained.

One run (three of the six first loads issued by ScalarE): 1308.67 us. The first rotation stands 7.62 us behind the stage's start instead of 8.05. But in the nine other executions that have all six loads on SyncE and B and C first it stands 7.4 to 8.5 behind it, so no gain is shown: theory B, or nearly.

### The edits together

> The changed kernel with five edits together: the own buffer for the first rounded angles, the scale's matmul ahead of the last group of linear terms, the gate loop split over VectorE, ScalarE and GpSimd, the first B and C loads issued from two queues, and the refinement of the root behind the rotations. Theory A: they add, since they stand in different stretches: 3.1 us (own buffer, as its run showed), up to 2.1 (scale matmul), 3.0 (split loop at 2.72 us a tile), 0.4 (two queues), 2.5 (boundary rounds from 20.74 back to 20.38): span 1290.7. Theory B: the preparation's chain is held by TensorE at its lower clock and by the store in front of VectorE's product, so that its edits don't add, and the span is 1296 or more.

Measured: 1295.33 us (1293.76 to 1295.54), ratio 0.9667 [0.9639, 0.9695]: faster than both kernels, 0.6% below the changed one, whose interval begins at 0.9704. Span 1293.6: next stage at 128.15 (4.9 earlier), first rotation 7.0 behind it (1.1 less), boundary rounds 20.38 and 20.62. The preparation's three edits, which should add to 8.2, gave 4.9, and the traces say where the rest is. The scales' matmul has nothing left to give: its 2.1 us of waiting are already part of what the own buffer takes away (0.03 in that run, 0.04 here). Of the own buffer's 3.1, 0.8 was its execution's own lead. The loop gives its 3.0, less 0.2 for a longer end and 0.2 for one more small operation ahead of it. 2.3 + 3.0 - 0.4 = 4.9; ahead of all these edits, at the first of L551, the two executions were within 0.2 us of each other. Theory A and B each hold for a part; 1293.6 lies between them.

## Why the prediction was right, point by point

- **Preparation, chain +6.3.** It was +9.1 (the quantising starts at 104.27, where the old chain ended near 95.1, ahead of the weight's two reductions, whose 0.6 only moved), and +7.6 to +12.4 over the seven executions with this preparation, +8.3 in the middle one. 1.2 of the miss is the rounding's wait for the store: the transposed copies start at 65.70, forecast 64.5. The other part is a wait that the prediction left out: VectorE's 2.14 us for the scales' matmul, which stands in TensorE's queue behind four groups of linear terms. I had costed VectorE's instructions and not the queue of the engine that they call on. The two are one chain: that queue is late because the copies are, and where the copies began at 59.4 or 60.1 the wait was 0.03.
- **Gate loop +24.8.** Exact, eight times 3.10, back to back; six of them taken out shortened the loop by 18.6. Rival 3 (5 us a tile by a round trip) is out. **End +2.3** was +1.8.
- **Start-up -10.6.** Measured -11.4, and right for a wrong reason: 5.4 us are the tables', 4.5 come from the stores that no longer stand ahead of the first loads, and 1.5 are left, most of it the size of the sines' table load. That the sum came out near is luck. The row to see it in was the first load itself: issued at 98.00 and used at 105.27, 7.3 us, while six loads of B and C were priced at 3.9 to land.
- **Steady stage -6.** Measured -0.4. The reductions: -8 taken, -6.0 measured; the prediction expected the return as waits for x, and most of it is the rotation's meeting with GpSimd's sums, a price that stood in its own rows ([rows 10], 1.06 instead of 0.74). Reciprocals and norm, +1.4 taken: +0.5 measured. The missing term: the refinement on GpSimd, +2.5, which the prediction priced in the closing but not at the boundaries, where it stands in GpSimd's queue ahead of rotations for which VectorE waits. GpSimd's products, +1.0 taken: +0.5, in odd tiles alone. The first round is +0.5. The fall of the clock, +1.5, has no term in the prediction either; the fourteen traces go with a tie to the refinement, but do not show it.
- **Rule on the shared port.** The prediction weighed the Trainium skill, SBUF — State Buffer, "Who interferes with whom", for the products, at 9 us; they cost 0.5. The trace agrees with the rule all the same, and the prediction had read the row of 1.06 us wrongly, as the price of a meeting. Every rotation that starts while one of GpSimd's 128x512 operations runs and has 0.2 us or more to go ends 0.55 us behind that one's end: 178 in the kernel before, 185 in the changed one, all within 0.01. So it lasts 0.75 when the other is nearly done, 1.07 when 0.5 us are left (354.52 + 1.07 is 355.04 + 0.55), and 1.77 when nearly all is. The products were cheap by their place: only in odd tiles does a rotation start well inside one (340.25, 1.05 us), and 0.2 of that was idle before. For the refinement it is GpSimd that stands: its four 128x4 operations beside rotations start 0.65 to 0.70 us apart and end 0.06 behind a rotation's end each time, and take 0.20 us in the closing, where VectorE is silent.
- **Rival 2** is out: seven more table loads brought no wait on the spread, and its Silu follows the load at once. By the Trainium skill, ScalarE: Activation LUTs, "What ACT_TABLE_LOAD costs", 1.4 us more would stand behind each; no run here shows them.

```profile
1162.81 1.28 ACT L1379 ACT_TABLE_LOAD   x1
1164.11 1.08 ACT L1379 ACTIVATE sz<-r 128x512 f32<-128x512 f32 x2
```

- **Rival 4** is out: the boundary's idle is 0.60 + 1.52 instead of 2.28. **Rival 5**: the place was right, the wait on the sum of squares is there in all seven tiles, 0.60 us at most, and inside the old idle.
- **Closing -57.8.** Exact: 7.2 us. GpSimd's four operations, taken at 1.2, took 1.1 with the gaps.

## What to carry to other kernels

When work leaves a saturated engine, price what it covered: here a third to two fifths of a removed operation came back, mostly as a longer meeting with another engine. When work is added to an idle engine, ask what stands behind it in that engine's queue and who waits for that; four operations on 128x4 cost the bound engine more (2.5 us) than two products on 128x512 at a better place (0.5). When edits are to be added up, ask whether one wait is counted in two of them. And test parts of a change one by one: of three parts here the overlap earned 24.5 of the 34.5 us, the move of the gate about 9, by what went with it, and the tables about one, too little for the medians to show.

## What was not expected of the hardware

- GpSimd's 128x4 operations take 0.57 to 0.62 us beside VectorE's two-input rotations and 0.19 to 0.20 without them. A rotation that starts with 0.2 us or more of a 128x512 GpSimd operation to go ends 0.55 us behind it, in all 363 cases of the two kernels' traces.
- The same preparation at the same busy TensorE was granted 2.4 GHz or 1.2 GHz from 34 to 48 us in different executions; the untouched one at 1.2 GHz began its next stage at 136.3, five at 2.4 GHz at 131.5 to 134.4. In the steady stage a fall of 3.4 us costs 1.5 to 1.6 us; profiled executions had from none to four of them, most in the round right behind a boundary, and there only where TensorE had just stood 1.43 us and not 0.77. What decides it beyond that was not settled; it is larger than most of the edits tested here. (Single rounds are 1.1 us longer without a fall, as at 1046 us without the refinement: there a spread lands 0.4 late and the rotation then meets GpSimd.)
- A load issued 0.6 us behind four stores of the cumulated rows was used after 6.8 to 7.3 us, and after 2.7 us without these stores just ahead.
